# A mixture-of-experts layer in a vision kernel: base term and token weights issued later, output banks in a new ring order

## The chip, the cores and the metric

The kernel runs on one core of a Trainium2 chip. The metric is the time of one execution on the device, in microseconds (us); lower is better. The engines are TensorE (PE in the profile, its weight loads PEld), VectorE (DVE), ScalarE (ACT), GpSimd (POOL) and SyncE (SP, which only issues transfers here). They run side by side and are ordered only by semaphores.

## The reference, cut to what matters

A tower of three layers over 32 images of 64 patches and a class token each, so 2,048 patch tokens and 32 class tokens of width 128. The first two layers (patch embedding and attention with relative positions) are untouched. The change is in the third, a layer of 8 experts of which each token uses two:

```
logits = xf @ Wr.T + br
probs = softmax(logits)
top2_prob, top2_idx = top_k(probs, 2)
comb = zeros((n, e)).at[arange(n)[:, None], top2_idx].add(top2_prob)
h = gelu(einsum('nd,edh->enh', xf, W1) + b1[:, None, :], approximate=False)
o = einsum('enh,ehd->end', h, W2) + b2[:, None, :]
y = einsum('ne,end->nd', comb, o)
out = h_in + y
```

The kernel computes all experts for all tokens. The part of `y` that comes from `b2` is `comb @ b2`; the kernel computes it apart and calls it the base term.

## The kernel before

The work is ordered by hand: each engine has one list of instructions, and semaphores named in the list `names` join them.

**Tokens and tiles.** `ALL` is 2,080 tokens. The up projection works with tokens along the free dimension, in 5 blocks of `FB` = 416 tokens; the down projection works with 128 tokens on the partitions, in 5 groups: four of 512 tokens (4 tiles) and one of the 32 class tokens.

**Up, `up(e, blk)`, line 1313.** For one expert and block it fills two banks of PSUM, one for each half `s` of the 256 hidden units, with three matmuls each (the operands are split in a high and a low part). The halves are counted by i = 10 e + 2 blk + s; `h_bank(i)` (line 218) gives the bank. Banks 0 to 3 are a ring, and i = 12 and 13 go to banks 5 and 6. `h_before(i)` (line 223) is how many gelus must be done before the bank may be written again.

**Gelu, `gelu(i)`, line 504, on ScalarE.** It empties that bank into `HB`, which has room for two experts, and counts `gelu_ok`. So for e of 2 or more it must not overwrite what the down projection of expert e - 2 still reads: at the first gelu of an expert it waits until all five down groups of expert e - 2 are done (`y2_ps`).

**Down, `down(e, g)`, line 1353, on TensorE; lines 969 to 980 on VectorE.** For one expert and token group, two matmuls per tile from `HB` and `w2_sb` into a bank of the output ring `out_bank(u)` = 4 + u % 4 (line 231), where u = `out_expert(e, g)` (line 227). VectorE then multiplies by the tokens' weights `comb` and adds to the accumulator `acc` (the buffer `KT`, which holds the residual), one instruction per tile, and counts `acc_ok`. The matmuls wait until the bank's last user, four places before in the ring, is evacuated. In the profile each float32 matmul of the program is two instructions, so an expert's five groups are 68.

**Router and base.** TensorE computes the logits in `router(n)`. VectorE takes the maximum off (up to `lg_ok`), ScalarE takes the exponential (line 522; its table is loaded before it, and the gelu table after it), and VectorE makes the weights `comb` (`comb_ok`, line 954). TensorE turns `comb` into bank 5 and 6 (lines 1375 and 1376), and ScalarE copies it to `combT` (lines 527 and 528, `cT_ok`). The base term is 17 small matmuls `base(c, g)` (line 1381) that contract over the 8 experts. They fill ring places 0 to 4, and VectorE adds each (lines 957 to 965, `base_ps`, `acc_ok`).

**The order on TensorE** is `up(0, 0)` to `up(0, 4)`, `up(1, 0)` to `up(1, 3)`, the transposes of `comb`, the base term's 16 matmuls, `up(1, 4)`, the class tokens' base matmul, and then for each expert e its five down groups and the five blocks of `up(e + 2, ·)`. On ScalarE the copies to `combT` stand between gelu 17 and gelu 18. On VectorE the five base additions stand before all down groups. SyncE sends the output when `acc_ok` reaches 41 to 45. No transfer is issued in the stretch that the change touches.

Of the kernel before, what the change touches and what calls it, by code (L numbers as in the profile page):

```python
# [8 lines left out]
ACT = mybir.ActivationFunctionType  # L9
# [4 lines left out]
P = 128  # L14
IMG = 32
NPATCH = 64
PAIRS = IMG // 2
TOK = IMG * NPATCH
C = 128
# [5 lines left out]
E = 8  # L25
# [51 lines left out]
def vit_kernel(nc, consts, x, cls_tok, W1_w, W1_b, W1_sw, W1_sb, W2_w, W2_b, W2_sw, W2_sb, W3_w, W3_b,  # L77
               eps_in1, eps_out1, eps_in2, eps_out2, Wq, bq, Wk, bk, Wv, bv, Wo, bo, rel_k, rel_v,
               Wr, br, fW1, fb1, fW2, fb2, out):
    with ExitStack() as ctx:  # L80
# [7 lines left out]
        bank = [banks[:, 512 * i:512 * (i + 1)] for i in range(8)]  # L88
# [3 lines left out]
        ident = kc[:, K_ID:K_ID + P]  # L92
# [17 lines left out]
        acc = KT[:, :].rearrange("p (t c) -> p t c", t=NT)  # L110
# [37 lines left out]
        b2s = sb("b2s", C)  # L148
# [27 lines left out]
        combT = vbd[:, 0:5 * P]  # L176
        combP = vbd[:, 5 * P:10 * P]
# [28 lines left out]
        S = {n: sem(n) for n in names}  # L206
# [19 lines left out]

        def out_expert(e, g):

            return 5 + 5 * e + g

        def out_bank(u):
            return 4 + u % 4
# [138 lines left out]
        def _(act):  # L371
            a = nc.scalar
# [99 lines left out]
            for i in range(1, PAIRS + 1):  # L472
# [4 lines left out]
                p = i - 1  # L477
# [6 lines left out]
                o = 8 * (p % 2)  # L484
# [6 lines left out]
                last = a.activation(SP[p % 4][:, 512:520], SP[p % 4][:, 512:520], ACT.Exp)  # L491
# [12 lines left out]
            def gelu(i):  # L504
                e, s, blk = i // 10, i % 2, (i // 2) % 5
                act.wait_ge(S["h_ps"], i + 1)
                if e >= 2 and i % 10 == 0:
                    act.wait_ge(S["y2_ps"], 5 * (e - 1))
                v = V_FB1 + 2 * e + s
                a.activation(HB[:, e % 2, s, blk * FB:(blk + 1) * FB], bank[h_bank(i)][:, 0:FB], ACT.Gelu,  # L510
                             bias=vecs[:, v:v + 1]).then_inc(S["gelu_ok"], 1)
# [9 lines left out]
            act.wait_ge(S["lg_ok"], 1)  # L521
            a.activation(lg[:, :], lg[:, :], ACT.Exp).then_inc(S["lexp_ok"], 1)
            a.preload_act_table_set("gelu_and_others")
            for i in range(8, 18):
                gelu(i)
            act.wait_ge(S["cT_ps"], 1)
            a.activation(combT[:, 0:4 * P], bank[5][:, :], ACT.Copy).then_inc(S["cT_ok"], 1)
            a.activation(combT[0:IMG, 4 * P:4 * P + IMG], bank[6][0:IMG, 0:IMG], ACT.Copy).then_inc(S["cT_ok"], 1)
            for i in range(18, 10 * E):
                gelu(i)  # L530

        @block.vector
        def _(dve):
# [422 lines left out]

            def base(u):

                dve.wait_ge(S["base_ps"], u + 1)
                if u < 4:  # L960
                    v.tensor_tensor(accv[:, :, u], bank[out_bank(u)].rearrange("p (g d) -> p g d", g=4),
                                    accv[:, :, u], ALU.add).then_inc(S["acc_ok"], 1)
                else:
                    v.tensor_tensor(acc[0:IMG, PAIRS, :], bank[out_bank(u)][0:IMG, 0:C], acc[0:IMG, PAIRS, :],
                                    ALU.add).then_inc(S["acc_ok"], 1)

            for u in range(5):
                base(u)
            for e in range(E):
                for g in range(5):  # L970
                    u = out_expert(e, g)
                    dve.wait_ge(S["y2_ps"], 5 * e + g + 1)
                    dve.wait_ge(S["acc_ok"], 5 if e == 0 else u - 4)
                    for i in range(4 if g < 4 else 1):
                        t = 4 * g + i
                        m = P if t < PAIRS else IMG
                        last = v.scalar_tensor_tensor(acc[0:m, t, :], bank[out_bank(u)][0:m, i * C:(i + 1) * C],  # L977
                                                      comb[0:m, t, e:e + 1], acc[0:m, t, :],
                                                      op0=ALU.mult, op1=ALU.add)
                    last.then_inc(S["acc_ok"], 1)  # L980

        @block.tensor
        def _(pe):
            t_ = nc.tensor

            def mm(o, l, r, start=True, stop=True):
                return t_.matmul(o, l, r, start=start, stop=stop)  # L987
# [325 lines left out]
            def up(e, blk):  # L1313

                for s in range(2):
                    i = 10 * e + 2 * blk + s
                    if h_before(i) > 0:
                        pe.wait_ge(S["gelu_ok"], h_before(i))
                    w = slice(e * FH + s * P, e * FH + (s + 1) * P)
                    t = slice(blk * FB, (blk + 1) * FB)  # L1320
                    o = bank[h_bank(i)][:, 0:FB]
                    mm(o, w1_hi[:, w], x_hi[:, t], True, False)
                    mm(o, w1_lo[:, w], x_hi[:, t], False, False)
                    mm(o, w1_hi[:, w], x_lo[:, t], False, True).then_inc(S["h_ps"], 1)
# [28 lines left out]
            def down(e, g):  # L1353


                need = min(5, ((g + 1) * BLK + FB - 1) // FB)
                pe.wait_ge(S["gelu_ok"], 10 * e + 2 * need)
                u = out_expert(e, g)
                pe.wait_ge(S["acc_ok"], u - 3)
                for i in range(4 if g < 4 else 1):  # L1360
                    t = 4 * g + i
                    m = P if t < PAIRS else IMG
                    for s in range(2):
                        last = mm(bank[out_bank(u)][0:m, i * C:(i + 1) * C], HB[:, e % 2, s, t * P:t * P + m],
                                  w2_sb[:, e, s, :], s == 0, s == 1)
                last.then_inc(S["y2_ps"], 1)

            pe.wait_ge(S["d_ffn"], 16)
            pe.wait_ge(S["gelu_ok"], 14)

            pe.wait_ge(S["comb_ok"], 1)
            pe.wait_ge(S["x2T_ok"], 5)
            pe.wait_ge(S["h1a_ok"], 2)
            for g in range(4):
                t_.transpose(bank[5][:, g * P:(g + 1) * P], combP[:, g * P:(g + 1) * P], ident)
            t_.transpose(bank[6][0:IMG, 0:IMG], combP[0:IMG, 4 * P:4 * P + IMG], ident[0:IMG, 0:IMG])\
                .then_inc(S["cT_ps"], 1)
            pe.wait_ge(S["d_small"], 112)
            pe.wait_ge(S["cT_ok"], 2)

            def base(c, g, m=P):

                r = slice(32 * c, 32 * c + E)
                o = bank[out_bank(c)][0:m, g * P:(g + 1) * P] if g < 4 else bank[out_bank(4)][0:m, 0:C]
                return mm(o, combT[r, g * P:g * P + m], b2s[r, :])

            for g in range(4):
                for c in range(4):
                    last = base(c, g)
                    if g == 3:  # L1390
                        last.then_inc(S["base_ps"], 1)
            up(1, 4)
            pe.wait_ge(S["acc_ok"], 1)
            base(0, 4, IMG).then_inc(S["base_ps"], 1)
            for e in range(E):
                for g in range(5):
                    down(e, g)
                if e + 2 < E:
                    for blk in range(5):
                        up(e + 2, blk)  # L1400
# [25 lines left out]
```

## Time and profile before

| | |
|---|---|
| runs | 274.6, 277.44 and 276.25 us; median 276.25 |
| profiled execution | 276.12 us; its span in the trace is 274.3 us |
| mean granted TensorE clock | 0.985 |
| busy: TensorE, VectorE, ScalarE, GpSimd | 243.3, 163.9, 129.6, 60.5 us |
| up matmuls (three groups of 80) | 29.9, 28.6 and 28.6 us busy |
| down matmuls (544) | 64.1 us busy |

The span is the time between the first and the last record of the execution; its own time is a little longer. Matmul records overlap, as TensorE is pipelined: a mean of 278 ns for a down matmul is not the distance from one start to the next. The line of a matmul is that of a helper (987), so they are told apart by the buffers they read: `w_all,region_d` is the down projection, `x_hi,w_hi`, `x_hi,w_lo` and `x_lo,w_hi` the up projection, `b2s,vbd` the base term and `kc,vbd` the transposes of the weights. `region_d<-banks` on ScalarE is a gelu, `vbd<-banks` a copy to `combT`.

### The profile page before, as it was taken

How to read it: one execution, taken by the hardware profiler on the slowest of the kernel's cores; microseconds unless marked ns; L12 is line 12 of the kernel's file. 1: busy time of each engine (PE TensorE's matmuls, PEld its weight loads, DVE VectorE, ACT ScalarE, POOL GpSimd, SP SyncE). 2: the span in 40 equal slices, each digit the busy share in tenths (PEclk: the TensorE clock that was granted, in tenths of full speed). 3: DMA queues.
4: the chain of work that ended last, by engine and by line, in shares of the span. 5: the costliest groups of instructions: out<-in, count | busy, mean ns of one | idle time of the engine just before them, and what ended most of it. 6: DMA issues, size and time to landing. Idle time of an engine off the chain costs nothing.

```text
span 274.3 us, 6405 instructions
## 1 busy us (share of the span) xinstructions
PE 243.3 (89%) x2519; PEld 209.3 (76%) x2519; DVE 163.9 (60%) x512; ACT 129.6 (47%) x432; POOL 60.5 (22%) x77
## 2 busy tenths in 40 slices
PE   0799997999886888895799978999999999999993
PEld 0665564899674656675689966999999999999993
DVE  0476888635679999999689463333333324242453
ACT  1543057942487999960015794052526262626100
POOL 8930122292023443563027000000000000000000
PEclk9999999999999999999999996899999999999998
DMA  6960000000000000270000000000000000000015
GB/s 218 279 142 2 1 0 0 2 4 2 0 0 4 2 2 2 88 223 5 5 2 0 4 0 0 2 0 0 2 0 0 2 1 2 0 4 0 0 25 133
DMA packets 6554, 7.95 MB, mean 29 GB/s; under 512 B 833, under 2 KB 5295, under 8 KB 6396
## 3 DMA queue, kind: packets, MB, share of 16 engines
q1 hardware_dynamic: 5260, 6.32, 8.2%
q10 hardware_dynamic: 720, 0.87, 1.2%
q0 software_dynamic: 544, 0.35, 0.5%
q8 instruction: 20, 0.33, 0.5%
q14 instruction: 10, 0.08, 0.1%
HBM read 6.47 MB, written 1.06 MB: 27 GB/s over the span
## 4 chain that ended last, share of the span: by engine, by line
PE 61%; DVE 24%; ACT 4%; DMA 4%; issue 3%; POOL 2%; ACTq 0%; DVEq 0%
PE banks L987 56%; DMA region_d<-in_L_tok_W_sw 4%; DVE stb L720 3%; DVE top L736 3%; DVE stb L640 2%; ACT region_d L510 2%; DVE stats L625 2%; DVE xnT L833 2%; PE banks L1186 2%; DVE region_c L761 2%; POOL rstd L309 2%; DVE mv L628 1%; DVE h L616 1%; DVE ntop L743 1%; DVE tmpx L828 1%
## 5 line engine op out<-in xcount | busy, mean ns | idle before, releaser
L977 DVE SCALAR_TENSOR_TENSOR KT<-banks,vbd,KT 128x128 f32<-128x128 f32 (+1 forms) x136 | 38.0, 344 | 61.1 <-PE banks L987 61.1
L510 ACT ACTIVATE region_d<-banks,vecs 128x416 f32<-128x416 f32 x80 | 45.6, 611 | 55.2 <-PE banks L987 55.2
L987 PE MATMUL banks<-w_all,region_d 128*128 128x128 f32 (+1 forms) x544 | 64.1, 278 | 0.0
L987 PEld LDWEIGHTS banks<-w_all,region_d 128*128 128x128 f32 (+1 forms) x544 | 62.2, 190 | 1.6 <-issue 0.6
L488 ACT ACTIVATE region_e<-banks,ntop 128x64 f32<-128x64 f32 x128 | 38.2, 326 | 7.0 <-DVE rsum L754 3.5
L987 PE MATMUL banks<-x_hi,w_hi 128*128 128x416 f32 x80 | 29.9, 373 | 0.9 <-ACT region_d L510 0.9
L987 PE MATMUL banks<-x_lo,w_hi 128*128 128x416 f32 x80 | 28.6, 358 | 0.0
L987 PE MATMUL banks<-x_hi,w_lo 128*128 128x416 f32 x80 | 28.6, 357 | 0.0
L488 ACT ACTIVATION_READ_ACCUMULATOR region_e<-banks,ntop 128x1 f32 x128 | 27.9, 218 | 0.0
L343 POOL TENSOR_TENSOR region_e<-region_e,rsum 128x512 f32<-128x512 f32 (+1 forms) x16 | 16.5, 1032 | 37.3 <-DVE rsum L754 37.3
L987 PEld LDWEIGHTS banks<-x_hi,w_hi 128*128 128x128 f32 x80 | 15.3, 191 | 2.8 <-issue 1.4
L1186 PE MATMUL banks<-kc,stb 128*128 128x128 f32 x64 | 10.4, 284 | 7.7 <-DVE stb L720 7.7
L987 PE MATMUL banks<-kc 128*128 128x128 f32 x70 | 10.0, 290 | 6.5 <-DMA kc<-in_consts 6.5
L987 PEld LDWEIGHTS banks<-x_lo,w_hi 128*128 128x128 f32 x80 | 15.3, 191 | 0.3
L987 PEld LDWEIGHTS banks<-x_hi,w_lo 128*128 128x128 f32 x80 | 15.3, 191 | 0.2
L987 PE MATMUL banks<-region_d,relk_bd 64*128 64x64 f32 x256 | 15.3, 288 | 0.0
L987 PEld LDWEIGHTS banks<-region_d,relk_bd 64*128 64x128 f32 x256 | 14.6, 188 | 0.6 <-issue 0.5
L987 PE MATMUL banks<-region_b,wnT 128*128 128x512 f32 x32 | 14.8, 599 | 0.0
L1186 PEld LDWEIGHTS banks<-kc,stb 128*128 128x128 f32 x64 | 6.8, 141 | 9.9 <-DVE stb L720 9.9
L987 PEld LDWEIGHTS banks<-kc 128*128 128x128 f32 x70 | 8.8, 199 | 6.7 <-DMA kc<-in_consts 6.5
L987 PE MATMUL banks<-region_c,RVBD 128*32 128x32 f32 x520 | 9.3, 239 | 4.7 <-issue 3.6
L987 PEld LDWEIGHTS banks<-region_c,RVBD 128*32 128x32 f32 x520 | 8.3, 126 | 5.5 <-issue 4.0
(219 smaller groups left out, 381.5 us busy)
## 6 DMA issues: line engine op xcount, KB each, us to landing
region_a<-in_x SPq DMA_DIRECT2D x2, 512.0 KB, 6.2
region_a<-in_x SPq DMA_DIRECT2D x1, 1024.0 KB, 11.0
w_sb<-in_L_ffn_W SPq DMA_DIRECT2D x1, 1024.0 KB, 5.6
out<-KT SPq DMA_DIRECT2D x8, 128.0 KB, 2.4
region_d<-in_L_attn_rel_v SPq DMA_DIRECT2D x2, 260.0 KB, 9.8
kc<-in_consts ACTq DMA_DIRECT2D x1, 336.0 KB, 5.7
region_d<-in_L_tok_eps_in ACTq DMA_DIRECT2D x2, 128.0 KB, 7.5
region_d<-in_L_tok_W_w ACTq DMA_DIRECT2D x1, 128.0 KB, 7.9
```

The source lines that it names most:

```text
L309: g.tensor_tensor(rstd[:, n * TPB:(n + 1) * TPB], ve[:, n * TPB:(n + 1) * TPB], mhalf[:, :], ALU.pow).then_inc(S["rstd_ok"], 1)
L343: g.tensor_tensor(ev, ev, rv, ALU.mult).then_inc(S["pn_ok"], 1)
L488: last = a.activation(dst[:, h // 2, h % 2], src[:, h // 2, h % 2], ACT.Exp, scale=SCALE, bias=ntop[:, o + h:o + h + 1], accum_out=esum[:, ...
L510: a.activation(HB[:, e % 2, s, blk * FB:(blk + 1) * FB], bank[h_bank(i)][:, 0:FB], ACT.Gelu, bias=vecs[:, v:v + 1]).then_inc(S["gelu_ok"], 1)
L625: last = v.bn_stats(stats[0:m, 6 * t:6 * t + 6], src[0:m, t * C:(t + 1) * C])
L640: last = v.tensor_scalar(ST[n % 2][0:m, i * C:(i + 1) * C], src[0:m, t * C:(t + 1) * C], mv[0:m, 2 * t:2 * t + 1], rstd[0:m, t:t + 1], ALU ...
L720: v.tensor_tensor(ST[p % 2].rearrange("p (g j m) -> p g j m", g=2, j=2), banks[:, 0:1024].rearrange("p (g h j m) -> p g h j m", g=2, h=2, ...
L736: most = mark(v.tensor_reduce(top[:, o].rearrange("p (j s) -> p j s", j=PJ), bank[2 + p % 2][:, :].rearrange("p (j k s) -> p j s k", j=PJ, ...
L761: v.tensor_copy(PT[:, :, 2 * p:2 * p + 2, 0:NPATCH], bank[4 + p % 2][:, :].rearrange("p (j b q) -> p j b q", j=PJ, b=2)).then_inc(S["pt_ok ...
L977: last = v.scalar_tensor_tensor(acc[0:m, t, :], bank[out_bank(u)][0:m, i * C:(i + 1) * C], comb[0:m, t, e:e + 1], acc[0:m, t, :], op0=ALU. ...
L987: return t_.matmul(o, l, r, start=start, stop=stop)
L1186: last = t_.transpose(bank[2 + p % 2][:, j * P:(j + 1) * P], ST[p % 2][:, j * P:(j + 1) * P], ident)
```

## The change

What it does:

- the ring of output banks is numbered anew: `down(0, 0)` and `down(0, 1)` have places 0 and 1, the transposes use the banks of places 2 and 3 (banks 6 and 7), the base term has places 4 to 8 (`out_base`), and all later groups n + 7. `out_done(u)` gives the count of `acc_ok` at which place u is evacuated;
- TensorE's order is now `up(1, 4)`, `down(0, 0)`, `down(0, 1)`, the transposes, `up(2, 0)`, base, `up(2, 1)`, the class tokens' base, `down(0, 2)`, `down(0, 3)`, `up(2, 2)`, `down(0, 4)`, `up(2, 3)`, `up(2, 4)`, and then the loop from expert 1 on. The 16 base matmuls wait for `acc_ok` 2 and count `base_ps` once instead of four times;
- ScalarE's copies to `combT` stand behind gelu 19 and read banks 6 and 7;
- a gelu of an expert e of 2 or more waits by block: at each block's first half for down group `blk` of expert e - 2;
- VectorE takes the first two down groups before the base additions, and waits for `comb_ok` at the first.

The diff:

```diff
--- before.py
+++ after.py
@@ -226,7 +226,15 @@
 
         def out_expert(e, g):
 
-            return 5 + 5 * e + g
+            n = 5 * e + g
+            return n if n < 2 else n + 7
+
+        def out_base(c):
+            return 4 + c
+
+        def out_done(u):
+
+            return u + 1 if u < 2 else u - 1
 
         def out_bank(u):
             return 4 + u % 4
@@ -504,8 +512,8 @@
             def gelu(i):
                 e, s, blk = i // 10, i % 2, (i // 2) % 5
                 act.wait_ge(S["h_ps"], i + 1)
-                if e >= 2 and i % 10 == 0:
-                    act.wait_ge(S["y2_ps"], 5 * (e - 1))
+                if e >= 2 and s == 0:
+                    act.wait_ge(S["y2_ps"], 5 * (e - 2) + blk + 1)
                 v = V_FB1 + 2 * e + s
                 a.activation(HB[:, e % 2, s, blk * FB:(blk + 1) * FB], bank[h_bank(i)][:, 0:FB], ACT.Gelu,
                              bias=vecs[:, v:v + 1]).then_inc(S["gelu_ok"], 1)
@@ -521,12 +529,12 @@
             act.wait_ge(S["lg_ok"], 1)
             a.activation(lg[:, :], lg[:, :], ACT.Exp).then_inc(S["lexp_ok"], 1)
             a.preload_act_table_set("gelu_and_others")
-            for i in range(8, 18):
+            for i in range(8, 20):
                 gelu(i)
             act.wait_ge(S["cT_ps"], 1)
-            a.activation(combT[:, 0:4 * P], bank[5][:, :], ACT.Copy).then_inc(S["cT_ok"], 1)
-            a.activation(combT[0:IMG, 4 * P:4 * P + IMG], bank[6][0:IMG, 0:IMG], ACT.Copy).then_inc(S["cT_ok"], 1)
-            for i in range(18, 10 * E):
+            a.activation(combT[:, 0:4 * P], bank[6][:, :], ACT.Copy).then_inc(S["cT_ok"], 1)
+            a.activation(combT[0:IMG, 4 * P:4 * P + IMG], bank[7][0:IMG, 0:IMG], ACT.Copy).then_inc(S["cT_ok"], 1)
+            for i in range(20, 10 * E):
                 gelu(i)
 
         @block.vector
@@ -956,21 +964,28 @@
 
             def base(u):
 
-                dve.wait_ge(S["base_ps"], u + 1)
+                dve.wait_ge(S["base_ps"], 1 + u // 4)
+                dve.wait_ge(S["acc_ok"], 2)
                 if u < 4:
-                    v.tensor_tensor(accv[:, :, u], bank[out_bank(u)].rearrange("p (g d) -> p g d", g=4),
+                    v.tensor_tensor(accv[:, :, u], bank[out_bank(out_base(u))].rearrange("p (g d) -> p g d", g=4),
                                     accv[:, :, u], ALU.add).then_inc(S["acc_ok"], 1)
                 else:
-                    v.tensor_tensor(acc[0:IMG, PAIRS, :], bank[out_bank(u)][0:IMG, 0:C], acc[0:IMG, PAIRS, :],
+                    v.tensor_tensor(acc[0:IMG, PAIRS, :], bank[out_bank(out_base(u))][0:IMG, 0:C], acc[0:IMG, PAIRS, :],
                                     ALU.add).then_inc(S["acc_ok"], 1)
 
-            for u in range(5):
-                base(u)
             for e in range(E):
                 for g in range(5):
                     u = out_expert(e, g)
+                    if (e, g) == (0, 2):
+                        for c in range(5):
+                            base(c)
                     dve.wait_ge(S["y2_ps"], 5 * e + g + 1)
-                    dve.wait_ge(S["acc_ok"], 5 if e == 0 else u - 4)
+                    if (e, g) == (0, 0):
+                        dve.wait_ge(S["comb_ok"], 1)
+                    if e > 0:
+                        dve.wait_ge(S["acc_ok"], max(7, out_done(out_expert(e - 1, g))))
+                    elif g >= 2:
+                        dve.wait_ge(S["acc_ok"], 7)
                     for i in range(4 if g < 4 else 1):
                         t = 4 * g + i
                         m = P if t < PAIRS else IMG
@@ -1356,7 +1371,8 @@
                 need = min(5, ((g + 1) * BLK + FB - 1) // FB)
                 pe.wait_ge(S["gelu_ok"], 10 * e + 2 * need)
                 u = out_expert(e, g)
-                pe.wait_ge(S["acc_ok"], u - 3)
+                if u >= 4:
+                    pe.wait_ge(S["acc_ok"], out_done(u - 4))
                 for i in range(4 if g < 4 else 1):
                     t = 4 * g + i
                     m = P if t < PAIRS else IMG
@@ -1365,34 +1381,44 @@
                                   w2_sb[:, e, s, :], s == 0, s == 1)
                 last.then_inc(S["y2_ps"], 1)
 
+            def base(c, g, m=P):
+
+                r = slice(32 * c, 32 * c + E)
+                o = bank[out_bank(out_base(c))][0:m, g * P:(g + 1) * P] if g < 4 else bank[out_bank(out_base(4))][0:m, 0:C]
+                return mm(o, combT[r, g * P:g * P + m], b2s[r, :])
+
+            up(1, 4)
             pe.wait_ge(S["d_ffn"], 16)
+            pe.wait_ge(S["lg_ok"], 1)
+            down(0, 0)
             pe.wait_ge(S["gelu_ok"], 14)
+            pe.wait_ge(S["h1a_ok"], 2)
+            down(0, 1)
 
             pe.wait_ge(S["comb_ok"], 1)
             pe.wait_ge(S["x2T_ok"], 5)
-            pe.wait_ge(S["h1a_ok"], 2)
             for g in range(4):
-                t_.transpose(bank[5][:, g * P:(g + 1) * P], combP[:, g * P:(g + 1) * P], ident)
-            t_.transpose(bank[6][0:IMG, 0:IMG], combP[0:IMG, 4 * P:4 * P + IMG], ident[0:IMG, 0:IMG])\
+                t_.transpose(bank[6][:, g * P:(g + 1) * P], combP[:, g * P:(g + 1) * P], ident)
+            t_.transpose(bank[7][0:IMG, 0:IMG], combP[0:IMG, 4 * P:4 * P + IMG], ident[0:IMG, 0:IMG])\
                 .then_inc(S["cT_ps"], 1)
+            up(2, 0)
             pe.wait_ge(S["d_small"], 112)
             pe.wait_ge(S["cT_ok"], 2)
-
-            def base(c, g, m=P):
-
-                r = slice(32 * c, 32 * c + E)
-                o = bank[out_bank(c)][0:m, g * P:(g + 1) * P] if g < 4 else bank[out_bank(4)][0:m, 0:C]
-                return mm(o, combT[r, g * P:g * P + m], b2s[r, :])
-
+            pe.wait_ge(S["acc_ok"], 2)
             for g in range(4):
                 for c in range(4):
                     last = base(c, g)
-                    if g == 3:
-                        last.then_inc(S["base_ps"], 1)
-            up(1, 4)
-            pe.wait_ge(S["acc_ok"], 1)
+            last.then_inc(S["base_ps"], 1)
+            up(2, 1)
+            pe.wait_ge(S["acc_ok"], 3)
             base(0, 4, IMG).then_inc(S["base_ps"], 1)
-            for e in range(E):
+            down(0, 2)
+            down(0, 3)
+            up(2, 2)
+            down(0, 4)
+            up(2, 3)
+            up(2, 4)
+            for e in range(1, E):
                 for g in range(5):
                     down(e, g)
                 if e + 2 < E:
```

## Rows read from the trace of the kernel before

**Rows 1.** The page: busy time, share of the span, instructions, of TensorE, VectorE and ScalarE

```profile
PE 243.3 (89%) x2519; PEld 209.3 (76%) x2519; DVE 163.9 (60%) x512; ACT 129.6 (47%) x432; POOL 60.5 (22%) x77
```

**Rows 2.** Chain of waits, 140 us to the end: start, us, what, count

```profile
159.52 1.28 ACT L523
160.80 0.01 issue
160.81 5.09 ACT region_d L510 x10
...
166.61 102.86 PE banks L987 x760
```

**Rows 3.** Table of stages: stretch, length, busy (instructions) per engine, granted clock, DMA share, GB/s

```profile
81.00:84.00 3.00, 1.36 (x14) 0.98 (x13) 2.83 (x13) 2.65 (x19) 1.21 (x2) 1.00 0.00 0
160.00:174.00 14.00, 11.29 (x74) 9.19 (x73) 7.08 (x20) 7.67 (x15) 0.00 (x0) 0.76 0.00 0
166.50:167.00 0.50, 0.39 (x9) 0.42 (x13) 0.00 (x0) 0.00 (x0) 0.00 (x0) 0.86 0.00 0
173.50:174.00 0.50, 0.50 (x5) 0.50 (x5) 0.00 (x0) 0.00 (x0) 0.00 (x0) 0.81 0.00 0
174.00:270.00 96.00, 96.00 (x713) 92.89 (x711) 37.16 (x133) 34.57 (x60) 0.00 (x0) 1.00 0.03 7
```

**Rows 4.** Timeline of TensorE, 161 to 180 us: start, length, instructions, [idle before, releaser]

```profile
161.47 0.46 PE L987 MATMUL banks<-x_hi,w_hi 128*128 128x416 f32 x1 [0.86 <-ACT region_d L510]
...
163.66 0.35 PE L987 MATMUL banks<-x_lo,w_hi 128*128 128x416 f32 x1
165.01 0.63 PE L1375 MATMUL banks<-kc,vbd 128*128 128x128 f32 x4 [1.01 <-ACT region_d L510]
165.57 0.20 PE L1376 MATMUL banks<-kc,vbd 32*32 32x32 f32 x1
166.61 1.91 PE L987 MATMUL banks<-b2s,vbd 8*128 8x128 f32 x32 [0.84 <-ACT vbd L528]
168.45 0.71 PE L987 MATMUL banks<-x_hi,w_hi 128*128 128x416 f32 x1
...
170.35 0.55 PE L987 MATMUL banks<-x_lo,w_hi 128*128 128x416 f32 x1
170.83 0.63 PE L987 MATMUL banks<-b2s,vbd 8*32 8x128 f32 x2
171.39 9.05 PE L987 MATMUL banks<-w_all,region_d 128*128 128x128 f32 x68
```

**Rows 5.** Timeline of VectorE, same columns: router's last step and base additions

```profile
164.50 0.30 DVE L954 TENSOR_TENSOR vbd<-rt 128x136 f32<-128x136 f32 x1
168.47 2.49 DVE L961 TENSOR_TENSOR KT<-banks,KT 128x512 f32<-128x512 f32 x4 [3.67 <-PE banks L987]
```

**Rows 6.** The page's group of all gelus: busy, mean ns of one | idle before

```profile
L510 ACT ACTIVATE region_d<-banks,vecs 128x416 f32<-128x416 f32 x80 | 45.6, 611 | 55.2 <-PE banks L987 55.2
```

**Rows 7.** Timeline of all engines, 180 to 194 us: one expert's cycle, same columns

```profile
180.37 0.45 PE L987 MATMUL banks<-x_hi,w_hi 128*128 128x416 f32 x1
...
180.66 0.35 PE L987 MATMUL banks<-x_hi,w_lo 128*128 128x416 f32 x1
...
180.85 0.35 PE L987 MATMUL banks<-x_lo,w_hi 128*128 128x416 f32 x1
...
186.19 7.86 PE L987 MATMUL banks<-w_all,region_d 128*128 128x128 f32 x68
188.18 1.13 DVE L977 SCALAR_TENSOR_TENSOR KT<-banks,vbd,KT 128x128 f32<-128x128 f32 x4 [6.88 <-PE banks L987]
189.96 1.13 DVE L977 SCALAR_TENSOR_TENSOR KT<-banks,vbd,KT 128x128 f32<-128x128 f32 x4 [0.66 <-PE banks L987]
...
193.98 0.45 PE L987 MATMUL banks<-x_hi,w_hi 128*128 128x416 f32 x1
```

**Rows 8.** Waits from 180 us to the end: who for whom, us, times, longest

```profile
ACT region_d L510 <- PE banks L987: 49.0, 6, 9.7
```

## The prediction

> **What bounds the kernel now.** The page first: TensorE is busy 243.3 us of the 274.3 us span, VectorE 163.9 and ScalarE 129.6 [rows 1]. A share over all stages does not say which wait ends last where the change acts, so next comes the chain of waits. Its last piece is one unbroken run of TensorE from 166.61 us for 102.86 us. Ahead of it stand ScalarE pieces: the load of the gelu table from 159.52 us, then ten gelus without a gap [rows 2]. So before 166.61 us ScalarE sets the time, and behind it TensorE alone does.
>
> The table of stages says what that costs. From 160 to 174 us TensorE is busy 11.29 us of 14 at a mean granted clock of 0.76; from 174 to 270 us it is busy all 96 us at 1.00 [rows 3]. The clock is still partly full in the slice from 166.5 us (0.86) and partly back in the one from 173.5 us (0.81). Between them it is 0.50, the 1.2 GHz level: from about 166.9 to 173.7 us, some 6.8 us.
>
> TensorE's own rows show three holes before that [rows 4]. It waits 0.86 us until 161.47, 1.01 us until 165.01 and 0.84 us until 166.61. The first is the ring of up banks behind the table load. The second ends when VectorE has finished the router's weights (start 164.50 us, 0.30 us long [rows 5]); ScalarE, which the row names, works through it without a break. The third is a round trip: TensorE turns the token weights, ScalarE copies them (the releaser named is line 528), and only then the base matmuls may start.
>
> From the second expert on there is nothing to gain. An expert's cycle lasts from 180.37 to 193.98 us, 13.61 us, without idle time [rows 7], and ScalarE waits for TensorE 49.0 us in total behind 180 us [rows 8].
>
> **The ledger before.** I take the stretch from 163.85 us, when the next matmul could have started (0.19 us behind the start of the last one of `up(1,3)` at 163.66), to 186.19 us, the first matmul of `down(1,0)` [rows 4, 7]. That is 22.34 us: wait 1.16; five transposes 0.70 (165.01 to 165.57, and 0.14 for the last); wait 0.90; base 1.84 (166.61 to 168.45); `up(1,4)` 2.38 (to 170.83); the class tokens' base 0.56 (to 171.39); the five down groups of expert 0 8.98 (to 180.37); `up(2,·)` 5.82.
>
> **The ledger after, part by part, at the full clock.** The same matmuls are issued, in another order.
>
> *`up(1,4)` moved ahead.* Its first half needs 15 gelus done, so the gelu i = 14. Ten gelus from 160.81 us last 5.09 us, one lasts 0.61 [rows 2, 6]: they start 0.498 us apart, so the seventh (i = 14) ends at 160.81 + 6 x 0.498 + 0.61 = 164.41 us. TensorE followed the ring's first release 0.05 us behind (gelu i = 8 ends at 161.42, matmul at 161.47). Wait 163.85 to 164.46: 0.61 us, where 1.16 was. The second half's gelu ends at 164.91 us, before it is wanted. Six matmuls 0.19 us apart (180.66 to 180.85 [rows 7]): 1.14 us, to 165.60 us.
>
> *`down(0,0)` and `down(0,1)` moved ahead of the transposes.* They need gelus and weights long there, and empty banks 4 and 5, which have no earlier user of the ring to wait for. A group lasts 1.78 us (VectorE starts on successive groups at 188.18 and 189.96 us [rows 7]): 3.56 us, to 169.16 us. The router's weights, ready at 164.80 us, are no longer waited for.
>
> *Transposes*, 0.70 us, to 169.86 us. *`up(2,0)`* behind them: 1.14 us and a switch from float32 matmuls to the narrower form. The switch has its price in the cycle: the last of the 68 down matmuls starts near 193.77 us and the next one at 193.98, and the first up matmul takes 0.29 us instead of 0.19. That is 0.1 and 0.1. So 1.34 us, to 171.20 us.
>
> *ScalarE's copies* hide under that. Before, base came 1.04 us behind the last transpose's start (165.57 to 166.61), so it is ready at 169.72 + 1.04 = 170.76 us: 0.44 us to spare. ScalarE has two more gelus ahead of the copies (i = 18 and 19), done near 166.9 us. Without this cover 0.90 us comes back.
>
> *Base's wait for both early groups' evacuation.* `down(0,1)` starts at 167.38 us; VectorE begins 1.99 us behind a group's first matmul (186.19 to 188.18) and takes 1.13: ready at 170.50 us, 0.70 to spare. Behind this VectorE wait stands only VectorE's own ring work, and VectorE is idle there.
>
> *Base at the full clock* is not in the trace; it ran nearly all at 0.50. Ends: 0.92 us (half of 1.84, all of it bound by the clock) and 1.84 (none). I take 1.40, to 172.60 us. The up matmuls halve with the clock (0.55 against 0.35 us long [rows 4, 7]), which speaks for the low end; the 32 small ones, 57 ns apart, against it.
>
> *`up(2,1)`* 1.24 us (the gap of its switch is inside base's figure), to 173.84; *the class tokens' base* between 0.28 and 0.56, taken as 0.40, to 174.24. It needs VectorE's first base addition; `down(0,2)` needs the second. VectorE starts where base ends (168.47 against 168.45 us), four additions last 2.49 us [rows 4, 5], so the second is done at 172.62 + 1.25 = 173.87 us, 0.37 to spare. If that cover is gone, each group waits up to one addition, 0.62 us.
>
> *The rest:* `down(0,2)` and `(0,3)` 3.56, `up(2,2)` 1.34, `down(0,4)` with its switch 0.65 (what the cycle's 7.79 us leave behind four groups), `up(2,3)` and `(2,4)` 2.38: to 182.17 us.
>
> *Ring order and waits in the steady part.* For e >= 1 a down group still waits for the group four places before it in the ring, with the same count of `acc_ok`: nothing. SyncE's output transfers wait for the same counts 41 to 45: nothing. No DMA moves, none is added. ScalarE's wait once an expert becomes one per block, 24 more. All ask for down groups that TensorE issued before the `up` in question, and ScalarE waits for TensorE anyway (49.0 us in 6 waits [rows 8]): nothing, down to where they make ScalarE slower than TensorE (below).
>
> **Sum.** 0.61 + 1.14 + 3.56 + 0.70 + 1.34 + 1.40 + 1.24 + 0.40 + 3.56 + 1.34 + 0.65 + 2.38 = 18.32 us, against 22.34: 4.02 us less. Of it 1.45 are waits and some 3.0 the clock; 0.4 go back in switches. The profiled execution took 276.12 us (span 274.3 and 1.8 around it), the median of the runs is 276.25. 276.12 - 4.02 = **272.1 us**.
>
> **Does the clock stay up?** The rows: it fell right behind the third of three holes within 6 us, the last two with only the transposes between them. It did not fall in a stretch where TensorE was busy 1.36 of 3 us (81 to 84 us [rows 3]). After the change only the first hole and 0.61 us are left, three microseconds apart, and from 164.46 us on TensorE does not stop. So I forecast 1.00 throughout.
> The Trainium skill (TensorE: Matmul & The Clock Gate, "HAM oscillation") ties the fall to a single long idle gap, and by it three holes of at most 1.01 us would not be the cause, so filling them would not return the clock. The trace disagrees, since it fell with no longer hole near it; by that rule the time would be that of the first rival.
>
> **The rivals.**
> 1. *The clock falls all the same.* Against: the rows above. For: the base matmuls use 8 rows each, the order now changes kind every few groups, and nothing in the trace shows such a mixture at full clock. Price: as long a stretch at half clock as before costs what it cost before, 2.6 (base not bound by the clock) to 3.4 us (6.8 / 2): about 272.1 + 3.2 = 275.3 us. Chance 0.12.
> The Trainium skill (the same page, "A second HAM failure mode: psum-queue depth-cycling") says that many small stops between groups that cycle through banks make the clock swing. The trace shows no swing in 96 us of cycling through eight banks.
> 2. *The waits move instead of going.* The covers are 0.44, 0.70 and 0.37 us thin. If ScalarE's copies and VectorE's additions each come late, TensorE waits 0.9 at base and 0.6 at `down(0,2)`: 273.6 us. For: three engines now hand over within 5 us. Chance 0.08.
> 3. *Slower: the gelus' waits by block.* Each new wait sits in ScalarE's queue ahead of a pair of gelus, for which TensorE waits three halves later. A pair takes ScalarE 1.00 us at best, TensorE 1.14. A wait dearer than 0.14 us makes ScalarE the bound, 30 blocks long (e = 2 to 7), so 276.25 x 1.01 is passed only if 30 x (w - 0.14) > 4.0 + 2.8, or w above 0.37 us. Against: the gap of issue ahead of ScalarE's ten gelus is 0.01 us [rows 2]. At w = 0.4 us: 279.9 us. Chance 0.03.
>
> The forecast keeps 0.77. Its own range is 270.6 (base at 0.92, switches free, a low run) to 273.8 (base at 1.84, class base at 0.56, a high run). For 8 in 10 it is widened towards the rivals: **270.3 to 274.3**. About 1% (2.8 us) is what a measurement of this kernel can tell from no change, its runs lying between 274.6 and 277.44; faster means below 273.5. Faster: 0.77 and half of the second rival, 0.82 with rounding; within 1%: the first rival and the other half, 0.15; slower 0.03.
>
> **What would show it.** Right: granted clock 1.00 from 160 to 182 us; one TensorE wait of about 0.9 us near 161, one of 0.6 near 164.5, no third; `down(1,0)` starting at 182.2 us instead of 186.2; cycles of 13.6 us behind. Wrong: a slice at 0.50 behind the transposes (rival 1); TensorE waiting for ScalarE's copy or VectorE's `KT` at base or `down(0,2)` (rival 2); gelus further apart than 0.58 us in `up(3,·)` and later, and TensorE waiting for them (rival 3). The sum also fails if base at the full clock lasts outside 0.9 to 1.8 us.

## The result

The changed kernel takes 271.68 us (median of 4 runs, 271.37 to 274.23) against 276.85 for the kernel before on the same chip: a ratio of 0.985, with a 95% interval of 0.980 to 0.989. Two later comparisons, on two different chips, gave a ratio of 0.989 (0.984 to 0.994) both times, 273.02 against 275.94 us and 272.63 against 275.89. The forecast was 272.1 us, in a range of 270.3 to 274.3. The profiled execution took 271.41 us, its span is 269.6.

The table of stages of the changed kernel answers to [rows 3]:

```profile
160.00:174.00 14.00, 12.70 (x106) 11.00 (x105) 8.09 (x26) 9.48 (x19) 0.00 (x0) 1.00 0.00 0
160.00:182.00 22.00, 20.70 (x162) 18.48 (x161) 11.44 (x36) 12.71 (x25) 0.00 (x0) 1.00 0.00 1
174.00:265.00 91.00, 91.00 (x678) 88.04 (x678) 35.46 (x126) 32.32 (x56) 0.00 (x0) 1.00 0.03 7
```

From 160 to 174 us the clock is 1.00 where it was 0.76, and TensorE is busy 12.70 us instead of 11.29. The 1.3 us without work up to 182 us are two waits. TensorE's timeline, which answers to [rows 4], shows them:

```profile
161.04 0.45 PE L1002 MATMUL banks<-x_hi,w_hi 128*128 128x416 f32 x1 [0.83 <-ACT region_d L518]
...
163.21 0.35 PE L1002 MATMUL banks<-x_lo,w_hi 128*128 128x416 f32 x1
164.03 0.46 PE L1002 MATMUL banks<-x_hi,w_hi 128*128 128x416 f32 x1 [0.47 <-ACT region_d L518]
...
165.28 3.73 PE L1002 MATMUL banks<-w_all,region_d 128*128 128x128 f32 x32
168.85 0.60 PE L1401 MATMUL banks<-kc,vbd 128*128 128x128 f32 x4
169.38 0.20 PE L1402 MATMUL banks<-kc,vbd 32*32 32x32 f32 x1
169.51 0.45 PE L1002 MATMUL banks<-x_hi,w_hi 128*128 128x416 f32 x1
...
170.84 1.17 PE L1002 MATMUL banks<-b2s,vbd 8*128 8x128 f32 x32
171.95 0.46 PE L1002 MATMUL banks<-x_hi,w_hi 128*128 128x416 f32 x1
...
173.28 0.40 PE L1002 MATMUL banks<-b2s,vbd 8*32 8x128 f32 x2
173.61 3.84 PE L1002 MATMUL banks<-w_all,region_d 128*128 128x128 f32 x32
177.20 0.43 PE L1002 MATMUL banks<-x_hi,w_hi 128*128 128x416 f32 x1
...
178.52 0.62 PE L1002 MATMUL banks<-w_all,region_d 128*32 128x128 f32 x4
179.07 0.46 PE L1002 MATMUL banks<-x_hi,w_hi 128*128 128x416 f32 x1
...
181.47 2.73 PE L1002 MATMUL banks<-w_all,region_d 128*128 128x128 f32 x23
```

A bracket is an idle time and what ended it. There are two: the wait of the ring behind the table load (161.04) and the shortened one at `up(1,4)` (164.03). Behind them is none: the transposes, base and the class tokens' base all start without a wait. ScalarE and VectorE, which answer to [rows 2, 5], show the covers at work:

```profile
160.38 6.09 ACT L518 ACTIVATE region_d<-banks,vecs 128x416 f32<-128x416 f32 x12
169.62 0.60 ACT L535 ACTIVATE vbd<-banks 128x512 f32<-128x512 f32 x1 [3.15 <-PE banks L1402]
170.12 0.17 ACT L536 ACTIVATE vbd<-banks 32x32 f32<-32x32 f32 x1
```

```profile
169.06 1.13 DVE L992 SCALAR_TENSOR_TENSOR KT<-banks,vbd,KT 128x128 f32<-128x128 f32 x4 [0.66 <-PE banks L1002]
172.09 2.48 DVE L970 TENSOR_TENSOR KT<-banks,KT 128x512 f32<-128x512 f32 x4 [1.90 <-PE banks L1002]
```

The copies end at 170.29 us and the second early group's evacuation at 170.19, both before base at 170.84. The second addition ends near 173.33 us, 0.28 us before `down(0,2)` wants it.

**One figure for the stretch.** The traces differ by up to 4 us in the stages ahead, which all the kernels here have alike (the first of the gelus behind the table load starts between 160.28 and 164.23 us), and by 1.4 us in the three traces of the changed kernel alone. So I compare traces by a distance that starts late: from the first of the gelus behind the table load to the first matmul of `down(1,0)`. It was 186.19 - 160.81 = 25.38 us and is 181.47 - 160.38 = 21.09 us, so 4.29 us less. What follows lasted 88.11 us (274.3 - 186.19) and lasts 88.13. The other 0.43 us of the span's 4.7 lie ahead of the change, where both kernels do the same: that part is not a gain. In all traces below the rest is 88.06 to 88.14 us; so whatever an edit does to a trace shows in this one distance.

### The profile page after: what moved, and what is told of

Read it like the earlier page. It is cut to its first block, busy times and chain, and to the rows that moved or that the text cites. A ratio compares the mean times of both kernels' runs of the same rounds, so it can differ in the third digit from the quotient of the medians.

```text
span 269.6 us, 6432 instructions
## 1 busy us (share of the span) xinstructions
PE 240.5 (89%) x2519; PEld 206.7 (77%) x2519; DVE 163.9 (61%) x512; ACT 129.5 (48%) x432; POOL 60.3 (22%) x77
## 4 chain that ended last, share of the span: by engine, by line
PE 61%; DVE 24%; DMA 4%; issue 3%; ACT 3%; POOL 2%; SPq 1%; DVEq 0%
PE banks L1002 55%; DMA region_a<-in_x 4%; DVE stb L728 3%; DVE top L744 3%; DVE stb L648 2%; DVE stats L633 2%; DVE xnT L841 2%; PE banks L1201 2%; DVE region_c L769 2%; ACT region_d L518 2%; POOL rstd L317 2%; DVE mv L636 1%; DVE h L624 1%; DVE ntop L751 1%; SPq L259 1%
## 5 line engine op out<-in xcount | busy, mean ns | idle before, releaser
L1002 PE MATMUL banks<-w_all,region_d 128*128 128x128 f32 (+1 forms) x544 | 63.3, 276 | 0.0
L1002 PEld LDWEIGHTS banks<-w_all,region_d 128*128 128x128 f32 (+1 forms) x544 | 61.3, 187 | 1.6 <-issue 0.5
```

## The experiments

| kernel | runs, us | before there | ratio (95%) | gelus to `down(1,0)`, us | clock in the stretch |
|---|---|---|---|---|---|
| before | 276.85 (276.12 in the profiled execution) | | | 25.38 | 0.50 for 6.8 us |
| before_2 | 275.47 (one) | 275.89 | | 23.76 | 0.50 for some 3.4 us |
| w_both | 273.64 | 275.94 | 0.992 (0.989 to 0.996) | 22.36 | 1.00 |
| w_third | 274.23 | 275.94 | 0.995 (0.992 to 0.998) | 22.46 | 1.00 |
| w_second | 275.57 | 275.89 | 0.996 (0.993 to 1.000) | 23.79 | 0.50 for some 3.4 us |
| up14_first | 275.07 | 275.94 | 0.998 (0.994 to 1.002) | 24.40 | 0.50 for some 3.4 us |
| changed (after_again, after_3) | 273.02, 272.63 | 275.94, 275.89 | 0.989 (0.984 to 0.994) | 21.08, 21.09 | 1.00 |
| no_cover | 272.67 | 276.33 | 0.987 (0.984 to 0.990) | 21.75 | 1.00 |
| old_gelu_waits | 272.98 | 276.33 | 0.989 (0.984 to 0.994) | 21.09 | 1.00 |
| dear_waits | 273.66 | 276.33 | 0.989 (0.984 to 0.994) | 21.09 | 1.00 |
| down_early (twice) | 270.58, 270.32 | 276.33, 275.89 | 0.980 (0.977 to 0.983), 0.980 (0.976 to 0.985) | 19.30, 19.31 | 1.00 |

**Is it the holes that let the clock fall?** Three kernels fill them with matmuls whose results nobody uses: `keep_warm(4)`, a helper of the kernel, issues four 128x128 matmuls, eight instructions in the profile. The edit of w_both to the kernel before (w_third has the second filler alone, w_second the first):

```diff
+            pe.wait_ge(S["x2T_ok"], 5)
+            keep_warm(4)
             pe.wait_ge(S["comb_ok"], 1)
-            pe.wait_ge(S["x2T_ok"], 5)
...
+            keep_warm(4)
             pe.wait_ge(S["d_small"], 112)
             pe.wait_ge(S["cT_ok"], 2)
```

> The kernel before with four idle-filling matmuls in the second and four in the third hole of TensorE (its results unused). Theory A, that the clock fell because of these holes: the waits stay (router's weights, copy to combT), the granted clock is 1.00 from 160 to 182 us, and only the clock's part of the gain comes, about 3 us less than before: 273.5 to 273.9 us against 276.85. Theory B, that the clock falls whatever the holes (by the kind of matmuls, or by a single long gap elsewhere): slices at 0.50 stay, and the time is 276.2 to 277.

Measured 273.64 us. TensorE's timeline of w_both, the first gelus on ScalarE's, and the table of stages:

```profile
163.82 1.13 PE L987 MATMUL banks<-kc 128*128 128x128 f32 x8
164.79 0.60 PE L1376 MATMUL banks<-kc,vbd 128*128 128x128 f32 x4
165.32 0.20 PE L1377 MATMUL banks<-kc,vbd 32*32 32x32 f32 x1
165.45 1.16 PE L987 MATMUL banks<-kc 128*128 128x128 f32 x8
166.54 1.17 PE L987 MATMUL banks<-b2s,vbd 8*128 8x128 f32 x32
167.64 0.46 PE L987 MATMUL banks<-x_hi,w_hi 128*128 128x416 f32 x1
...
168.99 0.40 PE L987 MATMUL banks<-b2s,vbd 8*32 8x128 f32 x2
169.32 7.97 PE L987 MATMUL banks<-w_all,region_d 128*128 128x128 f32 x68
...
182.99 1.28 PE L987 MATMUL banks<-w_all,region_d 128*128 128x128 f32 x10
```

```profile
160.63 5.09 ACT L510 ACTIVATE region_d<-banks,vecs 128x416 f32<-128x416 f32 x10
```

```profile
160.00:174.00 14.00, 13.17 (x118) 11.54 (x117) 8.77 (x27) 7.39 (x15) 0.00 (x0) 1.00 0.00 1
```

From the transposes to base it is 1.75 us (1.60 before, [rows 4]), so what TensorE waited for is no earlier. Only the clock is different, and the distance falls by 3.02 us, from 25.38 to 182.99 - 160.63 = 22.36. Theory A holds. The same work can be read off at both levels: base 1.10 us (166.54 to 167.64) against 1.84, the five down groups' record 7.97 against 9.05, of which the first 2.3 us were at half clock. The medians beside each other are 2.3 us apart and not 3.0, because the kernel before does not lose the same amount in every execution (before_2, below).

> The kernel before with four idle-filling matmuls in the third hole alone; the second, about 1.0 us, stays open. Theory A (the holes together make it fall): with 0.84 us of 1.85 filled the clock stays at 1.00 in most executions, 273.5 to 274.5 us. If the second hole alone is enough, or by theory B: 0.50 for some 7 us and about 276.5 us.

Measured 274.23 us, 22.46 us of distance, clock 1.00 in the stretch, as theory A had it. But this execution has a fall elsewhere, in the attention stage, which no kernel here changes:

```profile
81.00:84.00 3.00, 1.40 (x13) 0.94 (x12) 2.83 (x13) 2.63 (x19) 1.20 (x2) 1.00 0.00 0
84.00:91.00 7.00, 6.57 (x44) 4.79 (x46) 5.99 (x20) 5.05 (x35) 2.41 (x4) 0.52 0.02 5
```

The first line bears on the forecast. The same stage of the kernel before was as sparse, TensorE busy 1.36 of 3 us against 1.40 here, and no fall came behind it [rows 3]. So one execution without a fall does not show that a stage is safe.

Two others of the traces show a fall too (old_gelu_waits from about 131.5 us, dear_waits from about 137.7). So a fall is not bound to one place, and part of the scatter between runs of one kernel may be where, and how often, it comes.

> The kernel before with four idle-filling matmuls in the second hole alone; the third, 0.84 us, stays open. If the holes act together, the clock stays at 1.00 from 160 to 182 us, 22.4 us from the first of the ten gelus to down(1,0), and 273.6 to 274.3 us. If the third hole is enough: a slice at 0.50 there, 23.9 us or more, and about 276 us.

Measured 275.57 us, and the fall is there, later and shorter than in the first execution of the kernel before:

```profile
160.00:170.00 10.00, 8.29 (x73) 7.21 (x72) 5.36 (x18) 8.04 (x15) 0.00 (x0) 1.00 0.00 0
170.00:174.00 4.00, 4.00 (x19) 3.34 (x19) 2.06 (x5) 1.16 (x2) 0.00 (x0) 0.58 0.00 0
```

In this execution the fall came with the second hole filled; the first (0.86 us) and the third (0.85) were enough.

**Is the fall in every execution?** The mean granted clock is known for each run, not for the traced ones alone, though it does not say where a fall lay. The traces with 6.8 us at half clock (before, w_third) have a mean of 0.985 and 0.987, those with 3.4 us 0.990 to 0.994, those without a fall 0.996 to 1.000. All 44 runs of the kernel before in the three later comparisons have 0.992 or less. Of w_second's ten runs three have 0.997, and they are its three fastest (273.18 to 273.74 us); the other seven have 0.984 to 0.991 and took 275.00 to 277.36. Of w_third's ten runs six have 0.997 or more, of w_both's ten five (and a sixth 0.996), of no_cover's four all, and of the changed kernel's twelve eight. So the clock fell in every run of the kernel before, in the two traced ones in this stretch, and filling the third hole alone kept it up about as often as filling both.

**Was the profiled execution of before typical?**

> The kernel before, one more profiled execution: is the half clock from 166.9 to 173.7 us there in each of its executions? Theory A says yes in kind: a fall starts within some microseconds behind the transposes, and its length may differ. From the start of the ten gelus to the first matmul of down(1,0) it then takes more than 22.4 us (the figure with the holes filled) and up to 25.4 us, and 88.1 us follow. If no fall is there, the profiled execution was not typical and the clock is worth less than 3.0 us in the median.

The fall is there, but half as long:

```profile
160.00:169.00 9.00, 6.30 (x59) 5.22 (x58) 4.98 (x17) 7.43 (x15) 0.00 (x0) 1.00 0.00 0
169.00:173.00 4.00, 4.00 (x17) 3.08 (x17) 2.54 (x5) 1.21 (x2) 0.00 (x0) 0.57 0.00 0
```

The distance is 23.76 us. The clock cost 3.02 us in one execution of the kernel before and 23.76 - 22.36 = 1.40 us in the other. The changed kernel's 21.08 to 21.09 us thus stand against 23.8 to 25.4, a gain of 2.7 to 4.3 us, and the medians' distances of 2.9 and 3.3 us lie in it. The 5.2 us of the first comparison are more than the stretch gives in any trace; with four runs on each side and the scatter ahead of the stretch, its interval (0.980 to 0.989, or 3.0 to 5.5 us) includes smaller gains.

**One part alone.** `up(1,4)` ahead of the transposes, nothing else:

```diff
             pe.wait_ge(S["gelu_ok"], 14)
+            up(1, 4)
...
-            up(1, 4)
             pe.wait_ge(S["acc_ok"], 1)
```

> The kernel before with one edit: the last up block of expert 1 ahead of the transposes instead of behind base. The old ring and the old waits stay. Theory A: the second hole shrinks from 1.0 to 0.5 us, the third (0.84 us) stays, the clock stays up in most executions: 0.55 + about 3.0 us less than before, so 273.2 to 273.6 us. If the third hole alone lets the clock fall: 276.2. If the ring's new order or the gelus' waits by block carry part of the gain of the full change, this kernel lacks it and the rest of the distance to 271.7 us is more than the 0.9 us of the third wait.

It measured 275.07 us, no clear gain (0.994 to 1.002), and hit none of these figures. TensorE's timeline shows what I had left out:

```profile
165.28 0.43 PE L987 MATMUL banks<-x_hi,w_hi 128*128 128x416 f32 x1 [0.54 <-ACT region_d L510]
...
168.07 1.17 PE L987 MATMUL banks<-b2s,vbd 8*128 8x128 f32 x32 [0.84 <-ACT vbd L528]
169.98 0.40 PE L987 MATMUL banks<-b2s,vbd 8*32 8x128 f32 x2 [0.74 <-DVE KT L961]
170.67 9.57 PE L987 MATMUL banks<-w_all,region_d 128*128 128x128 f32 x68 [0.29 <-DVE KT L961]
```

`up(1,4)` behind base had covered VectorE's base additions. Moved away, it leaves two new waits for them, 1.03 us, against the 0.47 us won at the second hole (1.01 to 0.54). The clock falls in this execution for some 3.4 us (the table of stages of the same kernel):

```profile
172.00:175.00 3.00, 3.00 (x16) 3.00 (x16) 1.13 (x4) 0.00 (x0) 0.00 (x0) 0.50 0.00 0
```

In four of its ten runs the mean clock is 0.998, and these took 273.91 to 274.89 us, still above the 272.9 to 273.7 of w_both's runs at 0.997 or more: the new waits cost time without a fall too. The change put `up(2,1)` in that place, and the changed kernel shows neither wait.

**The cover between transposes and base.** `up(2,0)` behind base:

```diff
                 .then_inc(S["cT_ps"], 1)
-            up(2, 0)
...
             last.then_inc(S["base_ps"], 1)
+            up(2, 0)
             up(2, 1)
```

> The changed kernel with one edit: the first up block of expert 2 behind base instead of between the transposes and base. Theory A of the ledger: TensorE waits again for ScalarE's copy, 0.8 to 0.9 us at base, the clock stays at 1.00, everything behind starts 0.8 to 0.9 us later: about 272.5 us. Rival: that one hole of 0.9 us behind the transposes brings the half clock back, then 275 us or more.

```profile
169.04 0.60 PE L1401 MATMUL banks<-kc,vbd 128*128 128x128 f32 x4
169.57 0.20 PE L1402 MATMUL banks<-kc,vbd 32*32 32x32 f32 x1
170.57 1.17 PE L1002 MATMUL banks<-b2s,vbd 8*128 8x128 f32 x32 [0.80 <-ACT vbd L536]
```

The wait is back with 0.80 us, and 0.66 us arrive at the end of the stretch (21.75 against 21.09), less than the 0.8 to 0.9 expected: the two up blocks now stand together and take 2.47 us instead of 1.33 each. The clock holds, in the trace and by the mean in all four runs (0.997 or more), so in this order one such hole behind two down groups was not enough.

**The gelus' waits.** old_gelu_waits restores the wait once an expert for e > 2; dear_waits adds eight waits on a count long reached ahead of each block's first gelu (240 in all).

```diff
-                if e >= 2 and s == 0:
-                    act.wait_ge(S["y2_ps"], 5 * (e - 2) + blk + 1)
+                if e == 2 and s == 0 or e > 2 and i % 10 == 0:
+                    act.wait_ge(S["y2_ps"], 5 * (e - 2) + blk + 1 if e == 2 else 5 * (e - 1))
```

```diff
+                if e >= 2 and s == 0:
+                    for n in range(8):
+                        act.wait_ge(S["h1a_ok"], 1)
```

> The changed kernel with the gelus of experts 3 to 7 waiting once an expert as before; expert 2 keeps its waits by block, which its new order needs. Theory A: the waits by block cost and bring nothing, 271.4 to 272.0 us, with ScalarE idle some 7.9 us ahead of each expert as before. Rival 3 of the prediction (they are dear): faster than the changed kernel by a measurable amount.

> The changed kernel with eight more waits, all on a count long reached, ahead of the first gelu of each block from expert 2 on: 240 waits. It prices a wait. If one costs w us, the gelus of a block come 8 w later. Theory A: w is 0.02 us or so, so a pair of gelus takes 1.0 + 0.16 us, just at TensorE's 1.14, and the time is within 0.5 us of the changed kernel's. Rival 3: w near 0.1 or more, a pair takes 1.8 us, and each expert's up phase stretches by 5 x 0.66 less the ring's slack: 10 us or more slower.

The medians, 272.98 and 273.66 us, are both above what was expected, but the stretch is not: both have 21.09 us in it and 88.1 us behind it. An expert's ten gelus, ScalarE's timeline of the changed kernel and of dear_waits:

```profile
190.13 5.76 ACT L518 ACTIVATE region_d<-banks,vecs 128x416 f32<-128x416 f32 x10 [7.85 <-PE banks L1002]
```

```profile
193.98 5.76 ACT L521 ACTIVATE region_d<-banks,vecs 128x416 f32<-128x416 f32 x10 [7.85 <-PE banks L1005]
```

Ten gelus last 5.76 us either way, and ScalarE waits 7.85 us for TensorE ahead of them. As a pair still keeps up with TensorE's 1.14 us and takes 1.00 by itself, eight waits fit into 0.14 us or are hidden: at most 0.02 us each on the path, far from the 0.37 us of the third rival. The profiled executions took 271.92 and 275.24 us, and these 3.32 us lie ahead of the gelus, where the three kernels are alike: the first of the twelve gelus starts at 160.91 and 164.23 us, at 160.38 in the changed kernel's. That the medians differ for the same reason is likely, but only these executions show it.

**A version that beats both.** The remaining 0.83 and 0.47 us are filled by moving the first down group further ahead:

```diff
-            for blk in range(4):
-                up(1, blk)
+            up(1, 0)
+            up(1, 1)
...
-            up(1, 4)
             pe.wait_ge(S["d_ffn"], 16)
             pe.wait_ge(S["lg_ok"], 1)
             down(0, 0)
+            up(1, 2)
+            up(1, 3)
+            up(1, 4)
```

> The changed kernel with one edit: the first down group of expert 0 moved further ahead, between up(1,1) and up(1,2), where TensorE still waits 0.83 us behind the gelu table's load, with 0.47 us more at up(1,4). A group lasts 1.78 us, so both holes should go: 1.3 us less than the changed kernel, about 270.4 us. Rival: ScalarE's gelus, 0.50 us apart from 160.4 us on, set the pace up to up(1,4) whatever stands between, and the wait comes back further on: then 271.7 us.

> The changed kernel with the first down group between up(1,1) and up(1,2), again: 19.3 us from the first of the twelve gelus to down(1,0), so 1.8 us less than the changed kernel beside it. If the earlier distance of some 2 us was one of chips, the two are equal here.

> The changed kernel beside the next one, on the same chip: 271.4 to 273.0 us; 21.1 us from the first of the twelve gelus to down(1,0).

270.58 us, and in a second comparison 270.32 beside the changed kernel's 272.63; a ratio of 0.980 to the kernel before both times. Its table of stages and its timeline:

```profile
160.00:182.00 22.00, 22.00 (x175) 20.19 (x175) 12.11 (x38) 13.72 (x25) 0.00 (x0) 1.00 0.00 1
```

```profile
160.21 0.35 PE L1002 MATMUL banks<-x_hi,w_hi 128*128 128x416 f32 x1
160.77 1.95 PE L1002 MATMUL banks<-w_all,region_d 128*128 128x128 f32 x16
162.47 0.44 PE L1002 MATMUL banks<-x_hi,w_hi 128*128 128x416 f32 x1
```

TensorE no longer stops between 160 and 182 us. I expected 1.3 us, the sum of the two idle figures, and it was 1.79 (21.09 - 19.30). A hole costs more than its idle figure: the last matmul ahead of it runs out alone (it lasts 0.35 us where the next would have started 0.19 after it), so the two holes are 0.99 and 0.63 us, 1.62 in all. The other 0.17 us are in the matmuls around them, of which the first behind a hole takes 0.29 instead of 0.19. The changed kernel was also run again beside w_both, w_third and up14_first:

> The changed kernel again, beside the others on their chip: 271.4 to 272.0 us, granted clock above 0.99.

It took 273.02 us there, 1.0 above that range, so this one missed. The stretch has 21.08 us, and the trace's excess lies ahead of it (first gelu at 161.82 us against 160.38). The mean clock was 1.000 in the profiled execution, 0.994, 0.983 and 0.981 in the others; no trace shows where those falls lay.

## Why the prediction was right

**The sum.** It gave 18.32 us from the end of `up(1,3)` to `down(1,0)`; the trace has 18.07 (163.40 to 181.47). Term by term, forecast and measured: wait 0.61, 0.63; `up(1,4)` 1.14, 1.25; two down groups 3.56, 3.57; transposes 0.70, 0.66; `up(2,0)` 1.34, 1.33; base 1.40, 1.11; `up(2,1)` 1.24, 1.33; class tokens' base 0.40, 0.33; two down groups 3.56, 3.59; `up(2,2)` 1.34, 1.32; `down(0,4)` 0.65, 0.55; the last two blocks 2.38, 2.40. `down(1,0)` starts at 181.47 us where 182.17 was forecast: 0.25 us of that is the sum, 0.45 lies ahead of the stretch, in the scatter.

**Base was the one term that was clearly off.** I took the middle between its two bounds, 0.92 and 1.84, and it took 1.11 us. The low bound itself was wrong: it halves all of 1.84, but by the prediction's own reading the clock fell at 166.9 us, 0.3 us after base began at 166.61. With only the rest halved it is 0.3 + 1.54 / 2 = 1.07 us. So base is bound by the clock nearly in full, although its matmuls contract over 8 rows only, and the rows of before would have given the term to 0.04 us.

**The waits.** All three covers held: 0.55, 0.65 and 0.28 us to spare, against 0.44, 0.70 and 0.37. The price of the missing cover, put at 0.90 us, was 0.80 in no_cover. The second rival did not come about in this order, but up14_first shows that it was a real one: with `up(1,4)` gone from behind base in the old order, TensorE waited 0.74 and 0.29 us for VectorE, where I had said up to 0.62 for each group.

**The clock.** The forecast of 1.00 from 160 to 182 us was right in all three traces of the changed kernel, and the filler kernels show that the holes were the cause in the stretch: filled, the fall went, with everything else in place. One of its two reasons was weak: that no fall followed the sparse stage of 81 to 84 us was so in that execution, and not in w_third's. That the first rival's price would be 2.6 to 3.4 us was right for the profiled execution (3.02), and not for another one (1.40). The forecast time did not depend on that, because it was built up at full clock; the size of the gain did: 4.02 us was for an execution with the longer fall, and two comparisons of three gave 2.9 and 3.3. The Trainium skill (TensorE: Matmul & The Clock Gate, "HAM oscillation") ties the fall to a long idle gap; here it came with no gap longer than 1.01 us for some 30 us ahead of it (0.86 in w_second, 0.84 in up14_first), so no such gap was needed in this stretch, and the measurement decides. What the Trainium skill says on the same page of many small stops ("A second HAM failure mode: psum-queue depth-cycling") is nearer to what w_second and up14_first show.

**The gelus' waits.** Valued at nothing, and nothing is what taking most of them away or adding 240 did to the spans. Nor did the new ring order bring anything by itself: the rest of 88.1 us is the same to 0.08 us in all traces. It is what lets two down groups go ahead of base.

**What was luck.** The forecast lies 0.4 us from the median and 0.7 from the profiled execution, closer than the scatter ahead of the stretch allows one to expect. It was hung on one execution of the kernel before, and the traces differ by up to 4 us in those stages; the later medians of the changed kernel, 273.02 and 272.63 us, are within the stated range too, but not as near.

**What stays open.** Why one hole weighs more than another. By the mean clocks filling the second alone kept the clock up in three runs of ten and filling the third alone in six; no_cover's like hole behind two down groups did no harm in four. But ten runs are few, the mean does not place a fall, and the first hole was open in all of them. The fall's length (3.4 or 6.8 us) is not explained either.

## What to carry to other kernels

Build a forecast from start to start at the clock that the new order will have, not by taking idle figures off the profiled execution of before, which need not be a typical one. Where the clock falls within a record, halve only the part behind the fall. Ahead of moving a block of work into a hole, ask which other engine it was covering where it stood: moved alone, `up(1,4)` opened 1.03 us of waits at its old place and closed 0.47 at the new one. Where short holes stand close together on TensorE, the clock that they cost may be worth more than the waits (1.4 to 3.0 us here, against 22.36 - 21.09 = 1.3 for the waits).

## What the runs showed of the hardware that was not expected

- TensorE's clock fell to half with no idle gap above 1.01 us for some 30 us ahead of it, for about 3.4 us in three traces (before_2, w_second, up14_first) and 6.8 us in the first one of before.
- It is not settled by how sparse the stage ahead is: behind 81 to 84 us it held in the kernel before (TensorE busy 1.36 of 3 us) and fell in w_third (1.40 of 3).
- A hole in TensorE's work cost some 0.25 us more than its idle figure: two holes with 0.83 and 0.47 us gave 1.79 us when filled. 0.16 us of each is the last matmul running out.
- The 32 small base matmuls took 1.11 us at full clock and 1.84 with all but the first 0.3 us at half, although only 8 of their rows are used.
- Eight extra waits on a count long reached, ahead of each of 30 pairs of gelus, changed no span: 5.76 us for ten gelus with and without them.
